# Feed-forward layer in three split products: weights split by GpSimd during the attention, 39 unrolled slot tiles, results added by an accumulating scatter

## The reference

```python
x = x + _L0_xattn_ref(_layernorm(x), ctx_2048, W_fc, b_fc, W_q, b_q, W_k, b_k, W_v, b_v)
x = x + _L0_ffn_ref(_layernorm(x), gate_w, base_gate_up, base_down, expert_gate_up, expert_down)

def _L0_ffn_ref(x, gate_w, base_gate_up, base_down, expert_gate_up, expert_down):
    H, I, E, K = (256, 512, 8, 2)
    base_y = _silu_mul(x @ base_gate_up) @ base_down
    probs = softmax(xf @ gate_w)                 # 2048 tokens, 8 experts
    w, idx = top_k(probs, K);  w = w / w.sum(-1)
    comb = zeros((n, 8)).at[arange(n)[:, None], idx].add(w)
    for e in range(8):
        out = out + comb[:, e:e+1] * (_silu_mul(xf @ expert_gate_up[e]) @ expert_down[e])
    return out + base_y
```

## Time and profile before

| | |
|---|---|
| median of three runs | 1353.21 us |
| the profiled execution | 1355.13 us, span 1353.4 us |
| PE, PEld | 1261.2 us (93%), 872.1 us (64%) |
| DVE, ACT, POOL | 742.2 us (55%), 679.2 us (50%), 241.4 us (18%) |
| granted TensorE clock, mean | 0.974 |
| transfers | 168.36 MB, mean 124 GB/s |

### The profile page before, as it was taken

How to read it: one execution, slowest core, us unless ns; L and a number is a source line. 1 busy time by engine, 2 the same in 40 slices (tenths; PEclk the granted TensorE clock), 3 DMA queues, 4 the chain that set the end, 5 groups by cost and what they waited for, 6 DMA issues and landing times. The chain is left out here.

```text
span 1353.4 us, 22244 instructions
## 1 busy us (share of the span) xinstructions
PE 1261.2 (93%) x8100; PEld 872.1 (64%) x8101; DVE 742.2 (55%) x1550; ACT 679.2 (50%) x938; POOL 241.4 (18%) x236
## 2 busy tenths in 40 slices
PE   4699999999999999999999999999588999999992
PEld 3567777777777777777777777555235556666661
DVE  4256676767677667766767767777144111112213
ACT  3337666666666666666666666555331112222220
POOL 3311112111111111211111111000025402222121
PEclk9889999999999999999999999999889999999996
DMA  4656454565445645456544563450299201111115
GB/s 137 211 162 150 128 144 113 135 158 152 112 133 132 145 131 148 114 126 159 147 122 133 127 141 114 96 120 14 71 242 395 79 16 46 44 46 44 47 43 198
DMA packets 154910, 168.36 MB, mean 124 GB/s; under 512 B 69040, under 2 KB 140344, under 8 KB 154816
## 3 DMA queue, kind: packets, MB, share of 16 engines
q1 hardware_dynamic: 151360, 157.61, 44.5%
q0 software_dynamic: 3456, 9.47, 1.9%
HBM read 103.55 MB, written 63.31 MB: 123 GB/s over the span
## 5 line engine op out<-in xcount | busy, mean ns | idle before, releaser
L602 DVE TENSOR_REDUCE mx<-side 128x1 f32<-128x400 f32 (+1 forms) x1024 | 534.5, 570 | 139.9 <-PE side L454 130.8
L497 ACT ACTIVATE prob<-st 128x1024 f32<-128x1024 f32 (+1 forms) x416 | 411.8, 1023 | 183.2 <-PE st L475 182.1
L454 PE MATMUL side<-kst,qst 96*128 96x400 f32 (+1 forms) x1024 | 329.1, 382 | 3.7 <-DVE mx L602 2.4
L475 PE MATMUL st<-qst,kst 97*128 97x512 f32 (+1 forms) x832 | 265.0, 401 | 5.9 <-ACT prob L497 3.5
L454 PEld LDWEIGHTS side<-kst,qst 96*128 96x128 f32 x1024 | 189.6, 189 | 113.9 <-issue 37.5
L487 PE MATMUL acc<-prob,v 128*32 128x256 f32 (+1 forms) x3328 | 207.6, 385 | 0.0
L475 PEld LDWEIGHTS st<-qst,kst 97*128 97x128 f32 (+1 forms) x832 | 148.3, 186 | 18.2 <-ACT prob L497 8.9
L487 PEld LDWEIGHTS acc<-prob,v 128*32 128x32 f32 (+1 forms) x3328 | 95.7, 110 | 79.6 <-issue 24.4
L634 POOL TENSOR_TENSOR clo<-raw,chi 128x768 fp32r<-128x768 f32 (+1 forms) x32 | 60.8, 1901 | 450.0 <-ACT chi L528 450.0
L1429 DVE TENSOR_TENSOR hg<-sg,pu 128x512 f32<-128x512 f32 x40 | 27.5, 688 | 139.7 <-PE pu L1607 139.7
L640 POOL TENSOR_TENSOR flo<-fc,fhi 128x768 fp32r<-128x768 f32 (+1 forms) x32 | 61.1, 1910 | 214.8 <-ACT fhi L541 214.8
(11 more groups left out here) (162 smaller groups left out, 1407.1 us busy)
## 6 DMA issues: line engine op xcount, KB each, us to landing
kst<-parts_at SPq DMA_DIRECT2D x90, 400.2 KB, 5.8
parts_at<-parts SPq DMA_DIRECT2D x48, 384.0 KB, 5.9
v<-v_at SPq DMA_DIRECT2D x32, 408.0 KB
raw<-ctx_t SPq DMA_DIRECT2D x24, 384.0 KB, 3.3
v_at<-vst SPq DMA_DIRECT2D x32, 272.0 KB
wall<-gate_up SPq DMA_DIRECT2D x8, 1024.0 KB, 14.1
parts_at<-parts SPq DMA_DIRECT2D x16, 449.0 KB, 2.7
qst<-q_at SPq DMA_DIRECT2D x192, 32.0 KB, 5.9
```

Source lines behind the costliest of these rows:

```text
L454: pe.matmul(side[u.bank][:, 0:w], t.qst[0:96, pair, col * P:(col + 1) * P], t.kst[0:96, pair, o:o + w], start=True, stop=True).then_inc(si ...
L475: mm = pe.matmul(into[0:rows, i * 2 * NQ:(i + 1) * 2 * NQ], t.kst[0:97, GP * g + i, s * P:s * P + rows], t.qst[0:97, GP * g + i, :], start ...
L497: act.activation(prob[0:rows, s, :], st[(KT * g + s) % 2][0:rows, :], ACT.Exp, scale=float(DH) ** -0.5).then_inc(exp_done, 1)
L602: dve.tensor_reduce(mx[:, hq, r:r + 1], side[u.bank][:, 0:RANGES[r][1]], AX.X, ALU.max)\
```

## The change

The whole feed-forward layer is now computed as the attention's projections are, from split operands of type float32r in three products: high rows times high weights, high rows times low weights, low rows times high weights.

- **Weights.** During the attention SP loads the nine experts' weights in 27 pieces of 128x1024, one a phase; POOL copies a piece into its high part and subtracts (`pool_piece`); SP stores both to `w_at`. The feed-forward layer loads 24 KB a partition and expert from there: the shared expert and experts 0 to 2 (`EARLY`) from SP at its start, experts 3 to 7 from ACT's queue once all of `y` has been stored, since `wall` now fills the memory that `y`, `xh` and others held. A slot tile of such an expert waits for `late_in` against a register that PE reads from the tensor `need`.
- **Rows and hidden rows.** ACT writes the high part (`xh`, `hh`, `xgh`, `hgh`), DVE (POOL in the first chunk) subtracts for the low part (`xl`, `hl`, `xgl`, `hgl`).
- **Slot tiles.** 39 instead of 40, all written out, with rings of 5 for the input rows and 3 for the results, and two PSUM banks for the gate half.
- **Results.** `y`, the sum of the residual and the shared expert's result, is stored to a DRAM tensor `acc` (`token_sums`) of one row per token. Each slot tile's scatter adds its rows there (`compute_op=ALU.add`), and each such scatter waits for the one before. At the end `acc` is copied to `out` from DRAM to DRAM; the loads of two parts and DVE's additions are gone.
- **Empty slots.** `slot_x` is cleared by 13 transfers from POOL's queue during the attention, and not in the feed-forward layer. In `setup` SP also writes 128 rows of zeros to `acc`, behind `xrest`, and the block now waits for it.

```diff
@@ setup @@
                 sp.dma_start(t.xrest[:, :, :], tokens[:, QT:, :]).then_inc(t.x_rest_in, 16)
-                sp.wait_ge(small_in, 16 * (len(t.bias_in) + 2))
+                sp.wait_ge(empty_done, 2)
+                sp.dma_start(acc[N:N + P, :], t.empty[:, 0:D]).then_inc(small_in, 16)
+                sp.wait_ge(small_in, 16 * (len(t.bias_in) + 3))
@@ attention @@
+        def pool_piece(pool, p):
+            pool.wait_ge(piece_in, 16 * (p + 1))
+            pool.tensor_copy(piece_hi[:, :], piece[:, :]).then_inc(piece_hi_done, 1)
+            pool.wait_ge(piece_hi_done, p + 1)
+            pool.tensor_tensor(piece[:, :].bitcast(F32R), piece[:, :], piece_hi[:, :].bitcast(F32), ALU.subtract)\
+                .then_inc(piece_lo_done, 1)
...
+                        if 0 < p <= WEIGHT_PIECES:
+                            sp_store_piece(sp, p - 1)
...
+                        if p < WEIGHT_PIECES:
+                            sp_load_piece(sp, p)
...
@@ ffn, tiles on GpSimd @@
-                    pool.wait_ge(yg_done, RING * i + r + 1)
-                    pool.tensor_tensor(held[:, bass.ds(RING * i + r, 1)], half[0:1, 0:1], half[0:1, 0:1], ALU.add)
-                    pool.indirect_dma_start(
-                        out=part, out_offset=bass.IndirectOffsetOnAxis(ap=xg[r][:, D + 1:D + 2].bitcast(U32), axis=0),
-                        in_=yg[r][:, :], in_offset=None).then_inc(yg_out[r], 16)
+                pool.wait_ge(y_out, 16 * TC)
+                for n in range(SLOT_TILES):
+                    pool.wait_ge(yg_done, n + 1)
+                    after(pool, yg_out, 16 * n)
+                    pool.indirect_dma_start(
+                        out=acc,
+                        out_offset=bass.IndirectOffsetOnAxis(ap=xg[:, n % XG, D + 1:D + 2].bitcast(U32), axis=0),
+                        in_=yg[:, n % YG, :], in_offset=None, compute_op=ALU.add).then_inc(yg_out, 16)
@@ ffn, end on SP @@
-                for c in range(TC):
-                    for a, o in ((first_part, 0), (second_part, N)):
-                        sp.dma_start(a[:, c * TQ:(c + 1) * TQ, :],
...
+                sp.wait_ge(yg_out, 16 * SLOT_TILES)
                 for c in range(TC):
+                    sp.dma_start(out.rearrange("b q d -> (b q) d")[c * TW:(c + 1) * TW, :],
+                                 acc[c * TW:(c + 1) * TW, :]).then_inc(out_done, 16)
@@ ffn, tiles on ACT @@
+                turn_x(0)
+                act.wait_ge(y_out, 16 * TC)
+                for e in range(EARLY, E):
+                    load_expert(act, wall[:, e * W2:(e + 1) * W2], e, late_in)
+                for n in range(SLOT_TILES):
                     act.wait_ge(gate_full, n + 1)
@@ ffn, tiles on PE @@
+                def down_half(n, w):
+                    pe.wait_ge(hgl_done, n + 1)
+                    after(pe, yg_done, n)
+                    i = 0
+                    for a, part in ((hgh, 0), (hgh, WE), (hgl, 0)):
+                        for f in range(FT):
+                            mm = pe.matmul(py[1][:, 0:D], a[:, f, :],
+                                           wall[:, bass.ds(w * W2 + part + WD + f * D, D)],
+                                           start=(i == 0), stop=(i == 3 * FT - 1))
...
+                for n in range(SLOT_TILES):
+                    w = weights(n)
+                    loaded = pe.value_load(need[0:1, n:n + 1], min_val=1, max_val=1 + 16 * (E - EARLY))
+                    pe.wait_ge(xgl_done, n + 1)
+                    after(pe, sg_done, n - 1)
+                    pe.wait_ge(late_in, loaded)
+                    up_half(n, w, pg[n % 2], 0, gate_full)
+                    if n > 0:
+                        turn_h(n - 1)
+                    after(pe, hg_done, n)
+                    up_half(n, w, pu[0], I, up_full)
+                    if n + 1 < SLOT_TILES:
+                        turn_x(n + 1)
+                    if n > 0:
+                        down_half(n - 1, weights(n - 1))
@@ ffn, tiles on DVE @@
+                low_x(0)
+                for n in range(SLOT_TILES):
+                    if n > 0:
+                        low_h(n - 1)
+                    if n + 1 < SLOT_TILES:
+                        low_x(n + 1)
+                    product(n)
+                    if n > 0:
+                        scaled(n - 1)
```

More of the change, by code:

```diff
@@ L1426, in body, with product @@
+                def product(n):
                     dve.wait_ge(sg_done, n + 1)
                     dve.wait_ge(up_full, n + 1)
-                    after(dve, hg_turned, n, begin)
+                    after(dve, hg_turned, n)
                     dve.tensor_tensor(hg[:, :], sg[:, :], pu[0][:, :], ALU.mult).then_inc(hg_done, 1)
-                    if not begin:
-                        scaled(*before(i, r), first)
-                slot_tiles(dve, body)
-                scaled(ROUNDS - 1, RING - 1, False)
@@ L1513, in _ @@
+                turn_h(SLOT_TILES - 1)
             @block.tensor
@@ L1543, in _, with gate_up @@
                 mm.then_inc(lt_turned, 1)
-                pe.wait_ge(wb_in, 32)
+                def gate_up(c, f):
+                    n = FT * c + f
+                    after(pe, mul_done, n - 1)
+                    for dst, o in ((pg[f % 2], f * P), (pu[f % 2], I + f * P)):
+                        i = 0
+                        for a, part in ((xh, 0), (xh, WE), (xl, 0)):
+                            for k in range(KC):
+                                at = part + k * 2 * I + o
+                                mm = pe.matmul(dst[:, :], wb[:, at:at + P], a[:, k, c * TW:(c + 1) * TW],
+                                               start=(i == 0), stop=(i == 3 * KC - 1))
+                                i += 1
+                    mm.then_inc(g_full, 1)
@@ new lines, in counts, with down @@
+                def counts():
+                    pe.wait_ge(sel_done, 1)
+                    pe.wait_ge(consts, 3)
+                    sel_all = sel[:, :, :].rearrange("p t e -> p (t e)")
+                    pe.matmul(py[3][:, 0:T * E], below, sel_all, start=True, stop=True)
+                    pe.matmul(py[3][:, T * E:2 * T * E], ones, sel_all, start=True, stop=True)\
+                      .then_inc(count_full, 1)
+                def down(c):
+                    pe.wait_ge(hl_done, FT * (c + 1))
+                    for q in range(TQ):
+                        n = TQ * c + q
+                        after(pe, y_done, n - 1)
+                        i = 0
+                        for a, part in ((hh, 0), (hh, WE), (hl, 0)):
+                            for f in range(FT):
+                                at = part + WD + f * D
+                                mm = pe.matmul(py[q % 2][:, 0:D], a[:, f, q * P:(q + 1) * P], wb[:, at:at + D],
+                                               start=(i == 0), stop=(i == 3 * FT - 1))
+                                i += 1
+                        mm.then_inc(y_full, 1)
@@ L1585, in turn_x, with turn_h @@
                     mm.then_inc(xg_turned, 1)
[L1587 to L1588 removed]
+                def turn_h(n):
                     pe.wait_ge(hg_done, n + 1)
[L1590 removed]
+                    after(pe, hgl_done, n)
                     for f in range(FT):
@@ L1593, in turn_h @@
                     mm.then_inc(hg_turned, 1)
-                def down_half(i, r, first):
-                    n = RING * i + r
-                    w = weights(n)
-                    pe.wait_ge(hgt_done, n + 1)
-                    after(pe, yg_done, n, first and r == 0)
-                    for f in range(FT):
-                        mm = pe.matmul(py[1][:, 0:D], hgt[:, f, :], wall[:, bass.ds(w * WE + WD + f * D, D)],
-                                       start=(f == 0), stop=(f == FT - 1))
-                    mm.then_inc(yg_full, 1)
@@ L1605, in up_half @@
-                def up_half(r, w, dst, o, full):
-                    for k in range(KC):
-                        mm = pe.matmul(dst[:, :], xgt[r % 2][:, k, :], wall[:, bass.ds(w * WE + k * 2 * I + o, I)],
-                                       start=(k == 0), stop=(k == KC - 1))
-                    mm.then_inc(full, 1)
-                def body(i, r, first, last=False):
-                    n = RING * i + r
-                    begin = first and r == 0
-                    w = weights(n)
-                    pe.wait_ge(xgt_done, n + 1)
-                    after(pe, sg_done, n, begin)
-                    up_half(r, w, pg[0], 0, gate_full)
-                    if not begin:
-                        turn_h(*before(i, r), first)
-                    up_half(r, w, pu[0], I, up_full)
-                    if not last:
-                        turn_x(*behind(i, r), first and r + 1 < RING)
-                    if not begin:
-                        down_half(*before(i, r), first)
@@ new lines, in up_half @@
+                def up_half(n, w, dst, o, full):
+                    i = 0
+                    for a, part in ((xgh, 0), (xgh, WE), (xgl, 0)):
```

(6 more changed lines are left out.)

531 lines of the change are left out of this document (291 added, 240 removed).

## The result

Sixteen runs of the changed kernel have a median of 1358.16 us (1352.77 to 1362.33), sixteen of the kernel before beside them 1353.33 us. The ratio is 1.0032, 95% interval 1.002 to 1.0044: slower by 0.3%, where 1322 us and 31 us less were forecast. The time lay outside the range.

The account below looks back on a forecast made before the run. TensorE's stream bounds every long stage, if the other engines and its own sequencer keep up. Terms 5 + 2 + 1 - 17 - 10 - 12 = -31 us from 1353.2 gave 1322 us (50%), range 1308 to 1338, over the cases 1294 to 1348.

Parts of the forecast that it names:

- setup: Start of kernel: the small transfer behind `xrest` lands after it and all moves, +5 us, bounds 0 and +7.
- attention: POOL's added copies and subtractions and the larger transfers are mostly hidden: +2 us, bounds 0 and +15.
- passage and shared expert: Passage: DVE's 16 subtractions and three-product logits, +1 us; shared expert: shorter products less added waits, 74.3 us, -17 us.
- slot tiles: First addition to last scaled tile: period 5.6 us and two subtractions, -13 us; ACT's list +3 us; together -10 us.
- end: After the last scaled tile: last adding scatter and DRAM-to-DRAM copy take 12.7 us, -12 us, bounds -16 and -6.
- the addition's price: Slot tiles' adding scatters: +1 us for reading and adding in DRAM, bounds +0 and +3.6.
- The period: Slot tiles, gate half to gate half: 5.6 us instead of 5.82, held by PE's sequencer; bounds 5.03 and 6.0.
- the reads are hidden: Rival, 20%: in the slot tiles register reads cost nothing, the array bounds; period 5.03 us, 1300 us.
- The rival with 6.2 us a tile: Rival, 3%: slot tiles' register reads take the skill page's time, about 600 ns; period 6.2 us, 1345 us.
- The late loads: Slot tiles: during 39 us of late loads scatters take 6 to 8 us, rings hold two tiles; no cost.
- transfers collide: Rival, 15%: attention loses 12 us, or ACT's loads delay tiles by 12 instead of 3; 1340 us.
- the 3 us of the forecast: Slot tiles' start: SiLU of tile 0 behind `y` stores and five load issues, +3 us net, bounds +1 and +12.

Follow-up runs that it names:

- the kernel with the zeros first: 128 rows of zeros for `token_sums` sent ahead of `xrest`, against the kernel of "moving the reads"; ratio 0.9804, in another set 0.9769 (1318.89 us).
- fixed addresses: Each tile's expert written into the program, no register reads, one constant wait for late loads, against the changed kernel; 1320.75 us, ratio 0.9763.
- moving the reads: Next tile's reads of `expert` and `need` placed ahead of the down half's wait, against the changed kernel; 1326.07 us, ratio 0.9808.
- 4 KB rows: `w_at` laid out in pieces of 1024 columns instead of rows of 24 KB, against the kernel of "moving the reads"; ratio 0.9916.
- fine loads: Each late load cut into six 128x1024 transfers, three behind each SiLU of tiles 0 to 9, against "moving the reads"; 1323.04 us, 0.9775.
- the second set: Four kernels made from "moving the reads": short rows, late loads paced, zeros first, plain scatter; ratios 0.9916, 0.9954, 0.9804, 0.9875.
- the pairs above: Paced late loads with 4 KB rows (0.9753) against 24 KB rows (0.9954); plain scatter (0.9875) against adding scatter in "moving the reads" (0.9808).

## Why the prediction was wrong, by its steps

| step | forecast | measured in the profiles |
|---|---|---|
| setup | +5 | +4.6 |
| attention | +2 | -0.8 (last store of `x1` 970.88 to 974.72, +3.8 with the setup) |
| passage and shared expert | -16 | -13.7 (last addition 1092.4 to about 1082.5) |
| slot tiles | -10 | +22.3 (236.5 to 258.8) |
| end | -12 | -10.3 |
| span | -31 | +2.1 |

**Right.** The setup (confirmed by the kernel with the zeros first), the attention's cover, the end, the array's time in a tile (5.03 forecast, 4.99 with fixed addresses), the addition's price (+1 us forecast, +1.4 measured) and that it is covered in the steady tiles. The mechanism of the period was right too: PE's sequencer, held by the wait for `hgl_done`, late for the next gate half, with the idle time put down to "issue" and ended by moving the reads.

**The period, -8 us forecast in 38 tiles, +12 measured.** The forecast took two reads with their register instructions for 0.9 us and had the next gate half start at 5.55 us. The term was mis-sized: a read step takes 0.64 us in PE's sequencer (median of the tiles), so two take 1.3 us, +0.4. The rest, +0.1, is PE's release from the down half's wait at 3.54 us instead of 3.45 and the way to the first read. The earlier trace rows gave the durations of the two instructions of a read, but not the time between them; the distance of two starts would have. 38 x 0.5 us = 20 us. The bounds given (5.03 to 6.0) did not hold 6.13. The rival "the reads are hidden" asked for 5.03 us a tile and no idle time; it fell. The rival with 6.2 us a tile came out nearest, which is luck in part: it took the read itself for longer, but the read is 0.30 us and the step around it 0.64. The Trainium skill, page "DMA: Bandwidth & Descriptors", section on latency and other measured facts, gives about 600 ns as the floor of a tensor_load; the trace agrees for the whole step and not for the instruction.

**The late loads, "no cost" forecast for the scatters beside them, 13 to 14 us measured.** The step that failed is "During the 39 us of late loads it will be 6 to 8 us, but the rings hold two tiles in hand". The 6.0 us of the earlier trace rows came from scatters beside loads whose packets were nearly all under 8 KB (5066 of 5067); the new loads have rows of up to 24 KB. The first scatter took 14.8 us and the load of rows behind it 12.6, for which the forecast had no term (alone such a load takes about 2 us). Nor would the rings have held 6 to 8 us for nothing: with 4 KB rows and fine loads scatters landed in 5 to 9 us, and the gaps were smaller, not gone. The rival "transfers collide" allowed for 12 us in the tiles instead of 3, but put them on ACT's issue, which cost PE nothing until the rows were made short; the 3 us of the forecast did not come either.

**The shared expert, 2 us short.** The forecast had 3 us of open wait in its last chunk but nothing for the clock behind it. Between 1073.7 and 1079.1 us the down products stood 0.21 us apart instead of 0.12, some 25 of them, at the lower clock: about 2.4 us, an estimate from these distances.

Together: 20 us by the period, 14 by the gap and the slow tile behind it, less the 3 us that did not come, are 31 of the 32 us by which the slot tiles missed. By spans the whole sum missed by 33 us (-31 and +2.1); the shared expert and the end missed by 2 us each, and the attention gave 3 us back.

**Open.** What made ACT and DVE start late beside POOL's scatters in the profiles of the second set, and not in the others, was not found. The same kernel with zeros first did not show it in another set, and in the second set the kernel before was slower too, by about 7 us. How the cost of a scatter beside loads divides between the rows' length, the bytes under way and the addition is known only from the pairs above.

## What to carry to other kernels

Once a stream's products get shorter, count its sequencer as an engine of its own, by the distance between starts in the trace and not by the lengths of the instructions; and put reads of registers ahead of the wait that holds the sequencer, not behind it. Beside a bulk load a small transfer can take several times as long, the longer the bulk's rows the more: cut and pace the load, and keep its issue out of the chain that the array waits for.

## What the runs showed of the hardware

- A register read with its register instruction and check takes 0.64 us from start to start on PE's sequencer, although the two instructions are 0.30 and 0.15 us; in a tile whose sequencer was late, taking one away gave 0.66 us.
- An adding scatter of 128 rows of 1 KB lands in 3.8 us against 2.4 us for a plain one, and holds POOL for 1.56 us against 0.96.
- Beside five loads with rows of 24 KB on another queue such a scatter took 14.8 us, a plain one 8.2; beside one such load 9.9 to 12.4 us; beside rows of 4 KB 7.8 to 8.8 us; alone 3.8 us. Beside the long rows the bulk ran at 419 GB/s.
- Five loads of 768 rows of 4 KB in one go held ACT's issue for 19.6 us; five of 128 rows of 24 KB were issued in 2.6 us, one of 768 rows in 0.4 us.
- In a wait of PE of 2.84 us (up to 1073.35) the granted clock fell to 0.50 and stayed there until 1079.3, and eight float32r products of 256 columns took 2.08 us instead of 1.28.
